# Ten of sixteen comparison rows on ScalarE instead of eight, in the graph-building stage of a GNN kernel

## The chip, the cores and the metric

The kernel runs on one core of a Trainium2 chip. The metric is the device time of one execution in microseconds (us), median over runs; lower is better.

## What is computed

Four graph networks in a row over 6250 nodes and 100000 edges, each with a residual and a layer norm. All of them reduce to products of a feature matrix with one of two dense 6250 x 6250 matrices: W (sum of edge weights between two nodes) and C (number of edges between them).

```python
edge_index = jnp.stack([src, dst])          # dst is sorted
x = _layernorm(x + L0(x, edge_index, edge_weight, ...))   # three GCN layers: need W
x = _layernorm(x + L1(x, src, dst, ...))                  # SAGE: needs C
x = _layernorm(x + L2(x, edge_index, ...))                # five GRU steps: need C
x = _layernorm(x + L3(x, edge_index, ...))                # one GCN layer: needs C
```

## The kernel before

**Building the matrices** (`build_adjacency`). The edges are cut into NB = 49 batches of 2048, in an order ORDER that rises nearly with dst. An edge's cell (its place in the matrix) may occur twice in a batch, and then only one of the copies may be added, with the sum. So each batch is compared with itself: its 2048 keys stand in one row `krow` on all partitions, and for each of the 16 tiles j ("rows" in this text) the keys from tile j on are compared with the 128 keys of tile j, one per partition. Row j has (16 - j) * 128 elements, so row 0 has 2048 and row 15 has 128; row 6 has 1280 and row 7 has 1152. The results are masks `Eq`.

- VectorE (DVE) does rows 0 to DVE_ROWS - 1 in `compare`, one instruction each (L433). Before, DVE_ROWS is 8. Then it makes the one-hot matrices (L438, L443), masks the diagonal blocks of rows 0 to 7 (L450, the *first mask*), weights (L452), and masks the diagonal blocks of rows 8 to 15 (L455, the *second mask*), for which it waits for ScalarE's rows.
- ScalarE (ACT) does the other rows, each in two passes: square of the difference (L273, `distance`) and relu of one minus that (L281, `equality`). After a batch it waits until VectorE has done its rows (`row_used`), issues the load of the keys of the batch after next (L258), and goes on with the next batch.
- TensorE (PE) sums with the masks (L505, L508) and the one-hots (L511), once both masks are there.
- VectorE's `merge` (L463 to L472) turns the sums into the values and the addresses of the batch. It stands behind `compare` of the following batch.
- GpSimd (POOL) then issues 16 indirect DMAs per batch that add the values into W in HBM (L556, *adds*), each of 128 cells; ahead of a batch a small instruction, L531. The adds of all 49 batches into W come first, 782 in all, then in a second pass 782 into C.
- SyncE (SP) zeroes W and C at the start (L228), in zones of 512 columns, and GpSimd waits for the zones that a batch needs.

**The layers** (`run_layers`) follow on the same engines when `built` is set (L483). SP waits for that (L743) and streams the matrix through a ring of 9 buffers (L735); PE multiplies (L849). One stage goes over the matrix in four sweeps of 4, 3, 3 and 3 groups of 512 columns, 49 chunks each. In the first stage each of sweeps 0, 1 and 2 waits for the adds into W that touch its columns (L746), the last for all; in the first stage on C the same holds with the adds into C. Since dst is sorted and grows with the square of a uniform number, a column bound c covers the share sqrt(c / 6250) of the edges; worked out with the inputs and ORDER, sweep 0 needs the first 29 of the 49 batches, sweep 1 37, sweep 2 45 and sweep 3 all. Each sweep ends with L867 where a node adds itself.

Of the kernel before, what the change touches and what calls it, by code (L numbers as in the profile page):

```python
# [33 lines left out]
TB = 16  # L34
# [13 lines left out]
ORDER = [0] + [4 * g + u for g in range((NB - 5) // 4) for u in (2, 4, 1, 3)]  # L48
ORDER += [b for u in (0, 1) for b in range(len(ORDER) + u, NB - 1, 2)] + [NB - 1]
KEY_BIT = 0x50000000  # L50
DVE_ROWS = TB // 2

BANK = 512
UC = 4
# [95 lines left out]
def build_adjacency(nc, io, sems, persist, take, at, psum, c_added):  # L150
# [35 lines left out]
    total, more = take(P, [3, TB], F32), take(P, [TB], F32)  # L186
    apart = take(P, [2, (TB - DVE_ROWS) * P], BF16)
    mask = take(P, [TB], I32)
    names = "rows_in edges_in key_used ramps ident_set zero_set key_set keys_out far_set far_turned zones_set row_used " \
            "equal_set own_set apart_set late_rows batch_counted cell_set dve_step merged hot_set dump_zeroed x_pad_set needed_set needed_turned"  # L190
    s = {n: sems(n) for n in names.split()}
# [5 lines left out]
    def row_start(j):  # L197

        return j * EQ_PAIR if j < TB // 2 else (TB - 1 - j) * EQ_PAIR + (j + 1) * P
# [46 lines left out]
    def scalar(act):  # L246
# [17 lines left out]
        act.wait_ge(s["key_used"], 1)  # L264
        late = TB - DVE_ROWS

        def distance(b, u):

            j, slot = DVE_ROWS + u, b % 2
            n = b * late + u  # L270
# [5 lines left out]
        def equality(b, u):  # L276

            j, slot = DVE_ROWS + u, b % 2
            at = row_start(j)
# [59 lines left out]
    def vector(dve):  # L339
# [86 lines left out]
        def compare(b, slot):  # L426

            dve.wait_ge(row_in[slot], 16 * (b // 2 + 1))
            if b >= 2:
                dve.wait_ge(s["batch_counted"], b - 1)  # L430
            for j in range(DVE_ROWS):
                at = row_start(j)
                ins = dve.tensor_scalar(Eq[:, slot, at:at + (TB - j) * P], krow[:, slot, j * P:],  # L433
                                        keyf[:, b * TB + j:b * TB + j + 1], None, ALU.is_equal, ALU.add,
                                        accum_out=total[:, b % 3, j:j + 1])
            ins.then_inc(s["row_used"], 1)
            high, weighted = ohv[:, slot, :, 1, :], ohv[:, slot, :, 0, :]
            dve.tensor_tensor(high, psRamp[:, 0:CHUNKS].unsqueeze(1).to_broadcast([P, TB, CHUNKS]),  # L438
                              dhi[:, b * TB:(b + 1) * TB].unsqueeze(2).to_broadcast([P, TB, CHUNKS]),
                              ALU.is_equal).then_inc(s["hot_set"], 1)  # L440
            if b >= 1:
                dve.wait_ge(s["batch_counted"], b)
            dve.tensor_tensor(ohl, psRamp.unsqueeze(1).to_broadcast([P, TB, P]),  # L443
                              dlo[:, b * TB:(b + 1) * TB].unsqueeze(2).to_broadcast([P, TB, P]), ALU.is_equal)
            dve.wait_ge(s["row_used"], b + 1)

            half = TB // 2
            near = Eq[:, slot, 0:half * EQ_PAIR].rearrange("p (r f) -> p r f", f=EQ_PAIR)[:, :, 0:P]
            far = Eq[:, slot, EQ_FAR:EQ_FAR * (half + 1)].rearrange("p (r f) -> p r f", f=EQ_FAR)[:, :, 0:P]
            dve.tensor_tensor(Et[:, slot, 0:half, :], near, psUpto.unsqueeze(1).to_broadcast([P, half, P]), ALU.mult)  # L450
            dve.wait_ge(s["hot_set"], b + 1)
            dve.tensor_tensor(weighted, high, psW[:, b * TB:(b + 1) * TB].unsqueeze(2).to_broadcast([P, TB, CHUNKS]),  # L452
                              ALU.mult)
            dve.wait_ge(s["late_rows"], (b + 1) * (TB - DVE_ROWS))
            dve.tensor_tensor(Et[:, slot, half:, :], far, psUpto.unsqueeze(1).to_broadcast([P, half, P]),  # L455
                              ALU.mult).then_inc(s["equal_set"], 1)

        def merge(b, slot):
# [13 lines left out]
            dve.tensor_tensor(idx[:, at], mask, spare0[:, b % 2 * TB:(b % 2 + 1) * TB], ALU.bitwise_xor).then_inc(s["cell_set"], 1)  # L472

        compare(0, 0)
        for b in range(NB):
            if b + 1 < NB:
                compare(b + 1, (b + 1) % 2)
            merge(b, b % 2)
            if b == 0:
                conflicts()  # L480
# [1100 lines left out]
```

## Time and profile before

| | us |
|---|---|
| median of 3 runs (5507.01 to 5510.31) | 5510.14 |
| the profiled execution | 5502.16 |
| its span, first to last instruction | 5500.3 |
| busy: PE / DVE / ACT / POOL | 4752.6 / 1804.3 / 1189.9 / 2479.1 |

The span is that of the instructions; about 2 us of the execution's time lie outside it. The granted TensorE clock is 0.907 of full speed on average. The program has two parts that overlap: the build, until about 1100 us on VectorE and until about 3041 us on GpSimd, and the layers, from 1100 us to the end on TensorE. Idle time of an engine costs something only where another engine then waits for it.

### The profile page before, as it was taken

To read this page: it belongs to the slowest core of one execution; us is meant where nothing else is said; L and a number is where in the kernel's file an instruction comes from. 1 tells how busy PE (TensorE), PEld (TensorE's weight loads), DVE (VectorE), ACT (ScalarE), POOL (GpSimd) and SP (SyncE) were. 2 spreads that over 40 slices of the span, in tenths; PEclk is the share of its full clock that TensorE was granted. 3 is DMA by queue.
4 is the path that set the end of the run, shared out by engine and by line. 5 is a ranking of instruction groups with operands and counts; after the bars stand their busy time and mean duration, and the time that the engine had idled before them with its cause. 6 is when DMAs were issued, how large, how long until landed. Compare 5 with 4: busy or idle time off the path is not lost. (4 is left out here: it accounts for less than half of the span.)

```text
span 5500.3 us, 77896 instructions
## 1 busy us (share of the span) xinstructions
PE 4752.6 (86%) x25659; PEld 2555.6 (46%) x25659; DVE 1804.3 (33%) x3215; ACT 1189.9 (22%) x2478; POOL 2479.1 (45%) x1704
## 2 busy tenths in 40 slices
PE   3544545599699999999999899899999999999999
PEld 3544544544244444444454444444444444444444
DVE  9999999900001000110050211302113021130642
ACT  4555555411011111111120101202102021120320
POOL 3888888878878888888888100000000000000000
PEclk7555555599899999999999999999999999999999
DMA  9999993399699999999989787585775857758477
GB/s 359 369 365 336 341 302 48 31 336 285 179 287 300 274 301 288 296 276 298 288 232 266 225 272 238 154 297 191 244 252 180 299 185 252 244 184 298 144 229 249
DMA packets 717098, 1402.13 MB, mean 255 GB/s; under 512 B 268372, under 2 KB 356264, under 8 KB 691880
## 3 DMA queue, kind: packets, MB, share of 16 engines
q1 hardware_dynamic: 477388, 1342.89, 73.0%
q0 software_dynamic: 225216, 0.70, 7.9%
q10 hardware_dynamic: 14364, 56.99, 2.7%
q8 instruction: 58, 0.95, 0.1%
q14 instruction: 72, 0.59, 0.0%
HBM read 1160.09 MB, written 240.25 MB: 255 GB/s over the span
## 5 line engine op out<-in xcount | busy, mean ns | idle before, releaser
L849 PE MATMUL psum<-arena 128*128 128x512 f16 (+3 forms) x14014 | 3666.9, 422 | 103.9 <-issue 51.9
L849 PEld LDWEIGHTS psum<-arena 128*128 (+2 forms) x14014 | 1668.2, 123 | 2040.4 <-issue 961.9
L556 POOL DMA_INDIRECT W_adj<-arena x782 | 1211.1, 1549 | 279.2 <-issue 259.8
L556 POOL DMA_INDIRECT C_adj<-arena x782 | 1213.5, 1552 | 238.4 <-issue 238.4
L711 POOL TENSOR_TENSOR arena<-arena 128x512 f32 (+1 forms) x13 | 21.5, 1651 | 1716.6 <-DVE arena L1247 1716.6
L433 DVE TENSOR_SCALAR_CACHE_REDUCE arena<-arena 128x2048 bf16<-128x2048 f32 (+7 forms) x392 | 709.4, 1875 | 0.0
L505 PE MATMUL psum<-arena 128*128 (+1 forms) x6664 | 225.0, 167 | 545.3 <-DVE arena L455 523.4
L505 PEld LDWEIGHTS psum<-arena 128*128 128x128 bf16 x6664 | 214.3, 104 | 560.4 <-issue 506.6
L1443 DVE COPY arena<-psum 128x512 f32<-128x512 f32 (+1 forms) x39 | 23.2, 653 | 1174.0 <-PE psum L867 1174.0
L273 ACT ACTIVATE arena<-arena 128x1024 bf16<-128x1024 f32 (+7 forms) x392 | 298.4, 773 | 453.0 <-DVE arena L433 439.0
L1445 DVE TENSOR_SCALAR arena<-psum,arena 128x512 f32<-128x512 f32 x30 | 21.9, 748 | 1038.9 <-PE psum L849 1038.9
L511 PE MATMUL psum<-arena 128*128 128x98 f32 x1568 | 311.3, 390 | 1.5 <-issue 1.4
L1156 ACT ACTIVATE arena<-arena 128x128 f32 x432 | 127.7, 307 | 828.1 <-PE psum L849 808.1
L511 PEld LDWEIGHTS psum<-arena 128*128 128x128 f32 x1568 | 304.2, 302 | 1.6 <-issue 1.2
L281 ACT ACTIVATE arena<-arena 128x1024 bf16<-128x1024 bf16 (+7 forms) x392 | 297.5, 759 | 0.0
L1171 ACT ACTIVATE arena<-psum,arena 128x512 f32<-128x512 f32 (+1 forms) x48 | 28.5, 644 | 1062.5 <-PE psum L849 1062.5
L709 POOL COPY arena<-arena 128x512 f32 (+1 forms) x13 | 8.0, 614 | 502.1 <-DVE arena L1247 502.1
L802 PE MATMUL psum<-arena 128*128 (+1 forms) x260 | 139.4, 619 | 18.0 <-DVE arena L1342 8.8
L1364 DVE SCALAR_TENSOR_TENSOR arena<-psum,arena 128x512 f32 (+1 forms) x52 | 39.0, 751 | 310.5 <-ACT arena L1077 310.5
L804 PE MATMUL psum<-arena 128*128 (+1 forms) x260 | 135.0, 601 | 0.0
L1087 ACT ACTIVATE arena<-arena 128x128 f32 (+1 forms) x147 | 43.4, 307 | 403.2 <-PE psum L849 267.5
L508 PE MATMUL psum<-arena 128*128 128x1 bf16 x784 | 125.9, 165 | 1.4 <-issue 1.4
(236 smaller groups left out, 2571.3 us busy)
## 6 DMA issues: line engine op xcount, KB each, us to landing
arena<-C_adj SPq DMA_DIRECT2D x784, 384.0 KB
arena<-W_adj SPq DMA_DIRECT2D x294, 768.0 KB
arena<-C_adj SPq DMA_DIRECT2D x392, 512.0 KB
arena<-W_adj SPq DMA_DIRECT2D x147, 1024.0 KB
arena<-C_adj SPq DMA_DIRECT2D x392, 288.0 KB
arena<-W_adj SPq DMA_DIRECT2D x147, 576.0 KB
W_adj<-arena SPq DMA_DIRECT2D x12, 6400.0 KB
W_adj<-arena SPq DMA_DIRECT2D x12, 6144.0 KB
```

What stands on the lines that cost most here:

```text
L273: act.activation(apart[:, u % 2, 0:(TB - j) * P], krow[:, slot, j * P:], ACT.Square, bias=keyf[:, b * TB + j:b * TB + j + 1], scale=-1.0). ...
L281: act.activation(Eq[:, slot, at:at + (TB - j) * P], apart[:, u % 2, 0:(TB - j) * P], ACT.Relu, bias=one[:, 0:1], scale=-1.0, accum_out=tot ...
L433: ins = dve.tensor_scalar(Eq[:, slot, at:at + (TB - j) * P], krow[:, slot, j * P:], keyf[:, b * TB + j:b * TB + j + 1], None, ALU.is_equal ...
L505: pe.matmul(psS[:, slot, 5 * i:5 * i + 4], Eq[:, slot, block_of(j, i)], V[:, ds(b * TB + j, 1), :].rearrange("p a c -> p (a c)"), start=(i ...
L508: pe.matmul(psS[:, slot, 5 * i + 4:5 * i + 5], Et[:, slot, own_at(i), :], ones[:, 0:1], start=False, stop=(i == TB - 1), skip_group_check= ...
L511: ins = pe.matmul(psD[:, 0:2 * CHUNKS], ohl[:, j, :], ohv[:, slot, j].rearrange("p c k -> p (c k)"), start=False, stop=False, skip_group_c ...
L556: return pool.indirect_dma_start(table, bass.IndirectOffsetOnAxis(idx[:, t:t + 1], 0), values[:, t:t + 1], None, compute_op=ALU.add)
L802: pe.matmul(psum[:, 4 + gate, :], gates[:, gate * D:(gate + 1) * D], unit(sum_fm, j), start=True, stop=False)
L804: pe.matmul(psum[:, 4 + gate, :], wt[f"whhT{gate}"], unit(h_fm, j), start=False, stop=True).then_inc(s["probs_in"], 1)
L849: ins = pe.matmul(psum[:, bank + b, 0:width], lhs, ring[:, slot, b * BANK:b * BANK + width], start=begin and part == 0, stop=False, skip_g ...
L1087: act.activation(chunk32[:, slot, :], h_nm[:, at_, :].rearrange("p a f -> p (a f)"), ACT.Copy).then_inc(s["chunk_set"], 1)
L1156: act.activation(chunk32[:, u, :], h_nm[:, ds(i * LAP + (u + 1), 1), :].rearrange("p a f -> p (a f)"), ACT.Copy).then_inc(s["chunk_set"], 1)
```

## The change

VectorE takes rows 0 to 5, ScalarE rows 6 to 15. The first mask covers rows 0 to 7, so it now also reads two of ScalarE's rows and gets a wait for them. Nothing else is changed; buffers, the order of the engines' other work and the layers stay.

```diff
-DVE_ROWS = TB // 2
+DVE_ROWS = 6
@@ compare
             near = Eq[:, slot, 0:half * EQ_PAIR].rearrange("p (r f) -> p r f", f=EQ_PAIR)[:, :, 0:P]
             far = Eq[:, slot, EQ_FAR:EQ_FAR * (half + 1)].rearrange("p (r f) -> p r f", f=EQ_FAR)[:, :, 0:P]
+            dve.wait_ge(s["late_rows"], b * (TB - DVE_ROWS) + half - DVE_ROWS)
             dve.tensor_tensor(Et[:, slot, 0:half, :], near, psUpto.unsqueeze(1).to_broadcast([P, half, P]), ALU.mult)
```

On VectorE, in the first `compare` of the program (lines count one higher behind the new wait, so L450 of before is L451 now), the difference reads:

```order
 L433 TENSOR_SCALAR arena<-arena 128x1536
 L433 TENSOR_SCALAR arena<-arena 128x1408
-L433 TENSOR_SCALAR arena<-arena 128x1280
-L433 TENSOR_SCALAR arena<-arena 128x1152
 L438 TENSOR_TENSOR arena<-psum,arena 128x16x49
 L443 TENSOR_TENSOR arena<-psum,arena 128x2048
-L450 TENSOR_TENSOR arena<-arena,psum 128x1024 [waits row_used]
-L452 TENSOR_TENSOR arena<-arena,psum 128x16x49 [waits hot_set]
-L455 TENSOR_TENSOR arena<-arena,psum 128x1024 [waits late_rows]
+L451 TENSOR_TENSOR arena<-arena,psum 128x1024 [waits late_rows,row_used]
+L453 TENSOR_TENSOR arena<-arena,psum 128x16x49 [waits hot_set]
+L456 TENSOR_TENSOR arena<-arena,psum 128x1024 [waits late_rows]
```

Two comparisons are gone in each of 49 batches, and the first mask has one more wait.

On ScalarE the first batch began like this before (sizes are the elements per partition):

```order
L273 ACTIVATE arena<-arena 128x1024 [waits key_used]
L273 ACTIVATE arena<-arena 128x896
L281 ACTIVATE arena<-arena 128x1024 [waits apart_set]
L273 ACTIVATE arena<-arena 128x768 [waits late_rows]
L281 ACTIVATE arena<-arena 128x896 [waits apart_set]
```

and it begins like this now:

```order
L273 ACTIVATE arena<-arena 128x1280 [waits key_used]
L273 ACTIVATE arena<-arena 128x1152
L281 ACTIVATE arena<-arena 128x1280 [waits apart_set]
L273 ACTIVATE arena<-arena 128x1024 [waits late_rows]
L281 ACTIVATE arena<-arena 128x1152 [waits apart_set]
L273 ACTIVATE arena<-arena 128x896 [waits late_rows]
L281 ACTIVATE arena<-arena 128x1024 [waits apart_set]
```

Its two largest rows come first, ahead of those it had.

## Rows read from the trace of the kernel before

**Rows 1.** Windows, all engines: busy us (instructions) in each stretch, clock, DMA share, GB/s.
```profile
400.00:600.00 200.00, 102.09 (x1704) 99.35 (x1702) 199.07 (x250) 111.72 (x224) 165.22 (x114) 0.58 1.11 339
2000.00:2300.00 300.00, 295.76 (x846) 144.08 (x845) 16.23 (x40) 40.33 (x131) 250.58 (x171) 1.00 1.01 294
```
**Rows 2.** Timeline of PE: start, us, engine, line, operation, count [idle before, releaser].
```profile
1107.14 170.72 PE L849 MATMUL psum<-arena 128*128 128x512 f32 x392 [4.79 <-DMA arena<-W_adj]
...
1281.26 126.34 PE L849 MATMUL psum<-arena 128*128 128x512 f32 x294
...
1462.20 8.03 PE L849 MATMUL psum<-arena 128*128 128x512 f32 x13 [51.92 <-issue]
```
**Rows 3.** Timeline of PE at the first stage on C, last sweep.
```profile
3046.84 13.35 PE L849 MATMUL psum<-arena 128*128 128x512 f16 x70 [30.80 <-DMA arena<-C_adj]
```
**Rows 4.** Windows for L556 alone: POOL busy (adds), clock, DMA share, GB/s.
```profile
723.30:931.50 208.20, 173.44 (x112) 0.58 0.68 163
931.50:1158.50 227.00, 174.41 (x112) 0.66 0.50 123
```
**Rows 5.** Timeline of POOL around every 112th add into W.
```profile
723.40 1.55 POOL L556 DMA_INDIRECT W_adj<-arena  x1 [6.70 <-issue]
...
931.56 1.55 POOL L556 DMA_INDIRECT W_adj<-arena  x1 [0.30 <-issue]
...
1139.02 1.55 POOL L556 DMA_INDIRECT W_adj<-arena  x1 [0.16 <-issue]
1158.57 1.55 POOL L556 DMA_INDIRECT W_adj<-arena  x1 [18.00 <-issue]
...
1369.21 1.55 POOL L556 DMA_INDIRECT W_adj<-arena  x1 [2.77 <-issue]
```
**Rows 6.** Timeline of POOL: first batch, second batch, last add of the 45th.
```profile
70.37 1.72 POOL L556 DMA_INDIRECT W_adj<-arena  x1 [13.26 <-DVE arena L472]
...
106.09 0.19 POOL L531 TENSOR_TENSOR arena<-arena 128x1 f32<-128x1 f32 x1 [6.27 <-DMA W_adj<-arena]
...
1454.61 1.55 POOL L556 DMA_INDIRECT W_adj<-arena  x1 [0.30 <-issue]
```
**Rows 7.** Timeline of DVE: rows 6 and 7 of batch 0, end of its merge.
```profile
39.43 1.54 DVE L433 TENSOR_SCALAR_CACHE_REDUCE arena<-arena 128x1280 bf16<-128x1280 f32 x1
40.90 1.41 DVE L433 TENSOR_SCALAR_CACHE_REDUCE arena<-arena 128x1152 bf16<-128x1152 f32 x1
42.23 0.97 DVE L438 TENSOR_TENSOR arena<-psum,arena 128x784 f32<-128x784 f32 x1
...
69.89 0.18 DVE L472 TENSOR_TENSOR arena<-arena 128x16 int32<-128x16 int32 x1
```
**Rows 8.** Timeline of one batch in mid-build: DVE's L443 twice, PE's end.
```profile
606.52 2.28 DVE L443 TENSOR_TENSOR arena<-psum,arena 128x2048 f32<-128x2048 f32 x1
617.32 6.76 PE L511 MATMUL psum<-arena 128*128 128x98 f32 x32
628.16 2.28 DVE L443 TENSOR_TENSOR arena<-psum,arena 128x2048 f32<-128x2048 f32 x1
```
**Rows 9.** Timeline of ACT in the same batch, first and last instruction.
```profile
606.26 2.08 ACT L273 ACTIVATE arena<-arena 128x1024 bf16<-128x1024 f32 x2 [9.19 <-DVE arena L433]
...
618.42 0.18 ACT L281 ACTIVATION_READ_ACCUMULATOR arena<-arena 128x1 f32 x1
```
**Rows 10.** Groups by form, ACT, 60 to 1080 us: busy us, mean ns | idle before.
```profile
L281 ACT ACTIVATE arena<-arena 128x1024 bf16<-128x1024 bf16 x47 | 53.2, 1132 | 0.0
...
L281 ACT ACTIVATE arena<-arena 128x128 bf16<-128x128 bf16 x47 | 18.1, 385 | 0.0
```
**Rows 11.** Waits of SP, 750 to 1110 us: total, times, longest.
```profile
SPq L743 <- DVE arena L483: 287.5, 1, 287.5
```
**Rows 12.** Windows, all engines, while the layers stream W.
```profile
1130.00:1140.00 10.00, 10.00 (x25) 4.44 (x24) 0.00 (x0) 0.93 (x3) 8.62 (x7) 1.00 1.07 395
1390.00:1400.00 10.00, 10.00 (x25) 4.41 (x24) 0.00 (x0) 0.00 (x0) 8.62 (x7) 1.00 0.32 32
1450.00:1460.00 10.00, 0.00 (x0) 0.00 (x0) 0.00 (x0) 0.00 (x0) 8.56 (x7) 0.50 0.28 28
```

## The prediction

> **What bounds the kernel now.** I read the windows first. In the build VectorE is busy 199 of 200 us and GpSimd 165 of 200; later GpSimd keeps that density (251 of 300) while VectorE is nearly idle [rows 1]. That looks like a build bound by VectorE, and it is not. The windows of L556 alone, cut at every 112th add, give 208.2 us for 112 adds, which is seven batches of 16: 29.74 us a batch [rows 4]. VectorE's period, from L443 to L443 of the next batch, is 628.16 - 606.52 = 21.64 us [rows 8]. So VectorE runs ahead of the adds, and GpSimd is full in its own way: each add takes 1.55 us and 0.30 us follow it. Only its first batch waits for VectorE [rows 6].
>
> Then the timeline of PE, where the time is decided. The layers begin at 1107.14; the first two sweeps run to 1277.9 and 1407.6, and PE then stands still for 51.9 us until 1462.20 [rows 2]. The last add of the 45th batch is issued at 1454.61 [rows 6], and sweep 2 needs 45 batches: PE waits for GpSimd. It waits once more, 30.8 us until 3046.84, for the last sweep of the first stage on C [rows 3], which needs all 1564 adds. No wait behind that one is for an add. So the end of the kernel is the end of GpSimd's adds plus work that this change leaves alone. VectorE's gain counts only where it moves GpSimd.
>
> Last the timeline of GpSimd at its gaps. Between the first and the second add of batches 7, 14, 21, 28, 35 and 42, so after every 112 adds, it may pause. The idle time there is 6.70 us while SP zeroes (723.40), 0.30 us, so nothing, at 931.56 when the DMA is quiet, 18.00 us at 1158.57, and 2.77 us at 1369.21 while chunks stream evenly [rows 5]. The 18 us one falls into the burst with which SP fills the ring of nine 1 MB buffers: it may issue only when the build ends, at about 1102, and waits 287.5 us for that [rows 11], and until past 1150 the DMA moves some 395 GB/s [rows 12]. I read this as a pause for the adds in flight to land, which is long when they queue behind the burst. The fixed spacing speaks for it; the trace has only one such pause in a burst.
>
> **The change, part by part.**
>
> VectorE loses rows 6 and 7. Start to start they take 40.90 - 39.43 = 1.47 and 42.23 - 40.90 = 1.33 us [rows 7], so 2.80 us per batch and a period of 18.84. Over 49 batches its part of the build ends 137.2 us earlier.
>
> ScalarE gains two rows in two passes. An L281 of 1024 takes 1.132 us and one of 128 takes 0.385 [rows 10], so 0.107 us per 128 elements: 1.345 us for 1280 and 1.239 for 1152. L273 is like it, which makes 2 x 2.58 = 5.2 us, or 5.0 with the overlap of neighbours, on top of 618.60 - 606.26 = 12.3 [rows 9]: 17.3 us. That is dear per row, 5.0 against VectorE's 2.8 us. The Trainium skill ("ScalarE: Activation LUTs", Rules for kernel authors) advises VectorE over ScalarE for such plain arithmetic, and budgets about 0.3 us plus 0.83 ns per element; as an estimate that is 1.36 and 1.26 us and a batch of 17.5. With the page's figure too the batch stays under 18.84. ScalarE starts a batch 0.6 us after VectorE's rows of the one before (L443 at 606.52 less about 0.9 for L438, against 606.26, [rows 7 to 9]), so it ends at 17.9 of 18.84 us. Bounds: the two rows cost at least 4 x 1.13 = 4.5 us, and at most in proportion to tiles (19 more on 36) 6.5 us. At the upper end ScalarE sets a period of 19.4, still far under 29.74, and the build ends 25 us later than said.
>
> The new wait of the first mask. Rows 6 and 7 are ScalarE's first, done some 6.5 us after it starts (the two passes and the square of row 8). VectorE comes to the mask after six rows that are each longer than 1.47 us, 8.8 at least, and L438 and L443, 3.1 more. Behind the wait stand the weights, the second mask, the merge and so GpSimd, but it is over by 5 us or more each time. Cost: nothing. The second mask waits for all ten rows. Counted from the end of VectorE's rows of the batch before, L443 starts at 0.9 + 18.84 = 19.7 us and the mask stands 2.2 us and more behind it; ScalarE is done at 17.9.
>
> PE ends batch work at 624.08, and VectorE comes to L443, which waits for it, at 628.16; 2.80 us earlier is 625.36, so 1.3 us remain [rows 8]. No cost; and if it had one, it would be the build's, which has 10.9 us a batch to spare against the adds.
>
> GpSimd's start. Two `compare` stand ahead of the first merge: 2 x 2.80 = 5.60 us. The first add comes at 64.8 in place of 70.37. The zones were ready at 57.1 (70.37 - 13.26), so nothing else stops it. The waits of batches 1 and 2 are for the landing of the batch before (6.3 us, [rows 6]) and move along. **Gain 5.6 us.** Bounds: 0 if the early landings, among the zeroing, are later; 5.6.
>
> The pause after 112 x 5 adds. The layers now begin at 1107.14 - 137.2 = 969.9; the 29 batches that sweep 0 needs are in by then (batch 28's last add stands 14 adds of 1.85 behind 931.56, at 957.5, less 5.6). Sweep 0 takes 170.7 us, to 1140.6. Its loads end earlier: sweep 1's were over by about 1391, since 1390 to 1400 moved only 32 GB/s, 16 us before PE's 1407.6 [rows 2, 12]. So the DMA is quiet from about 1124, because sweep 1 must wait for batch 36. GpSimd comes to its pause 5.6 us before the old place, at 1135, 11 us into the quiet. The pause should be that of 931.56: 0.30 in place of 18.00. **Gain 17.7 us.** Bounds: with the loads still running, 2.77, a gain of 15.2; in the burst, none.
>
> The burst itself moves to 965, where 0.30 at 931.56 (926 now) is already past. Sweep 1 waits for batch 36, whose last add stands 30 adds of 1.855 behind 1158.57, at 1214.2, less 23.3 now; PE follows such an add by 7.6 us (1454.61 and 1462.20, [rows 2, 6]), so near 1199, and ends near 1326; the next pause, at 1369.21 less 2.5 and less 23.3, is at 1343: quiet too. **Gain 2.5 us.** Sweep 2 and everything on C keep their place relative to the adds.
>
> Sum: 5.6 + 17.7 + 2.5 = 25.8 us. Against the profiled execution, 5502.16 - 25.8 = 5476.4; that execution is 8 us under the median of the runs, so against the median 5510.14 - 25.8 = 5484.3 us. PE waits much more in the first stage (for batch 36 as well) and is at the lower clock when it starts again, but it was so before sweep 2 also (0.50 at 1450, [rows 12]), and the adds, not PE, decide.
>
> **Rivals.**
>
> *A, the 18 us belong to the burst, not to the count.* Too many adds in flight stop GpSimd wherever the burst is; then they only move to about 1005. Gain 5.6 + 2.5 = 8.1: 5502.0 us. For it: one case only. Against: the gap sits exactly at the 112th add. Chance 0.17.
>
> *B, the pause meets a part of the streaming*, because ScalarE or PE ends the build later by over 11 us: 5.6 + 15.2 + 0 to 2.5, so 5487 to 5489; if the build ended only 10 to 25 us earlier than before, it would still meet the burst. With A's mechanism in part, up to 5498. Chance 0.10.
>
> *C, slower.* As A, and the backlog also stops GpSimd in the new burst at sweep 1, which is filled from empty where it followed seamlessly before: 18 us more. Then -5.6 - 2.5 + 17.7 = +9.6, 5519.7 us. It decides from a third pause of over 8 us. Against it: sweep 2 starts from empty before, and the adds behind 1462 keep their 1.85 us. Chance 0.04.
>
> *D, the saving is hidden wholly*: the usual reading, "VectorE is not the bound", with the pause unchanged and the early gain lost among the zeroing: 5508 to 5512. Chance 0.04.
>
> **How the numbers follow.** The forecast has 0.65, with 5478 to 5492 for the sum and the spread of the medians. B adds 0.10 up to 5498. A is within 0.2% (11 us, about what a measurement of this kernel can tell from no change), D too; C lies at the edge of slower. Faster: 0.65 + 0.10 less a little for spread: 0.74. Same: 0.17 + 0.04 + 0.01: 0.22. Slower: 0.04. The range reaches from 5476 to 5504, so it holds A and leaves out C and D and what goes beyond the sum.
>
> **What would show it.** VectorE's L443 should come every 18.8 us; ScalarE's group of a batch should take 17 to 18 us. The first add should start near 65 us and PE's first L849 near 970. The pause behind the 560th add should be under 1 us near 1135, with PE waiting near 1141 to 1199 and 1326 to 1436. The wait for C should end near 3021. It is wrong if a gap of 10 us or more stands elsewhere among the adds, or if PE has no wait for C at all, so that another chain sets the end.

## The result, and the profile after

The changed kernel takes 5477.36 us (median of 5 runs, 5475.12 to 5479.92) against 5507.13 us of the kernel before (5505.86 to 5510.31): ratio 0.9944, 95% interval 0.993 to 0.9959, 29.8 us faster by the medians. The profiled execution took 5476.16 us, 26.0 us less than that of before (5502.16); 25.8 were forecast.

The timeline of PE in the changed kernel (start, us, then what stood idle before), which answers to [rows 2] and [rows 3]:

```profile
969.73 170.15 PE L850 MATMUL psum<-arena 128*128 128x512 f32 x392 [5.29 <-ACT arena L1088]
...
1196.36 129.12 PE L850 MATMUL psum<-arena 128*128 128x512 f32 x294 [52.91 <-issue]
...
1434.14 46.02 PE L850 MATMUL psum<-arena 128*128 128x512 f32 x103 [105.98 <-issue]
...
3021.89 38.44 PE L850 MATMUL psum<-arena 128*128 128x512 f16 x227 [31.71 <-DMA arena<-C_adj]
```

The layers start 137.4 us earlier, and PE loses most of it standing: 52.9 us before sweep 1 and 106.0 before sweep 2, where one wait of 51.9 was before, so 107.0 of the 137.4. At the last sweep of the first stage on C the gain is down to 3046.84 - 3021.89 = 24.95 us.

The timeline of GpSimd, for [rows 5] and [rows 6]:

```profile
65.00 1.72 POOL L557 DMA_INDIRECT W_adj<-arena  x1 [7.92 <-DVE arena L473]
...
716.86 1.55 POOL L557 DMA_INDIRECT W_adj<-arena  x1 [3.77 <-issue]
...
924.99 1.55 POOL L557 DMA_INDIRECT W_adj<-arena  x1 [0.30 <-issue]
...
1133.11 1.55 POOL L557 DMA_INDIRECT W_adj<-arena  x1 [0.30 <-issue]
...
1341.24 1.55 POOL L557 DMA_INDIRECT W_adj<-arena  x1 [0.30 <-issue]
...
3015.92 1.55 POOL L557 DMA_INDIRECT C_adj<-arena  x1 [0.30 <-issue]
```

The pauses of 18.00 and 2.77 us in batches 35 and 42 are gone: 0.30 us stand there, as ahead of every add. The windows around them (PE, PEld, DVE, ACT, POOL busy, clock, DMA share, GB/s), for [rows 12]:

```profile
1000.00:1010.00 10.00, 10.00 (x24) 4.38 (x24) 0.00 (x0) 0.93 (x3) 8.47 (x6) 1.00 1.08 398
1116.00:1126.00 10.00, 10.00 (x25) 4.39 (x24) 0.00 (x0) 0.00 (x0) 8.17 (x7) 1.00 0.33 33
1130.00:1140.00 10.00, 10.00 (x27) 4.51 (x26) 0.00 (x0) 0.08 (x1) 8.62 (x7) 1.00 0.23 2
```

The burst is where the layers start now (398 GB/s at 1000), and when GpSimd comes to batch 35 the DMA moves 2 GB/s. In the burst itself GpSimd is not held: its adds go on at their pace (six begin in these 10 us). Rival A had put a stop of 18 us there.

One batch of mid-build on VectorE and ScalarE, for [rows 8] and [rows 9]; two timelines:

```profile
595.14 2.35 DVE L433 TENSOR_SCALAR_CACHE_REDUCE arena<-arena 128x2048 bf16<-128x2048 f32 x1
...
613.89 2.35 DVE L433 TENSOR_SCALAR_CACHE_REDUCE arena<-arena 128x2048 bf16<-128x2048 f32 x1
```

```profile
607.37 2.51 ACT L273 ACTIVATE arena<-arena 128x1280 bf16<-128x1280 f32 x2 [1.14 <-DVE arena L433]
...
624.80 0.19 ACT L281 ACTIVATION_READ_ACCUMULATOR arena<-arena 128x1 f32 x1
```

VectorE's period is 613.89 - 595.14 = 18.75 us, ScalarE's batch 624.99 - 607.37 = 17.62. ScalarE waits 1.14 us for VectorE where it waited 9.19.

### The profile page after: what moved, and what is told of

Same layout as the page of the kernel before. It is cut to its first block and busy times, and to the rows that moved or that the text cites. A ratio compares the mean times of both kernels' runs of the same rounds, so it can differ in the third digit from the quotient of the medians.

```text
span 5474.4 us, 78043 instructions
## 1 busy us (share of the span) xinstructions
PE 4734.8 (86%) x25659; PEld 2543.3 (46%) x25659; DVE 1667.5 (30%) x3019; ACT 1444.8 (26%) x2772; POOL 2476.9 (45%) x1704
## 3 DMA queue, kind: packets, MB, share of 16 engines
q0 software_dynamic: 225216, 0.70, 7.9%
## 5 line engine op out<-in xcount | busy, mean ns | idle before, releaser
L506 PE MATMUL psum<-arena 128*128 (+1 forms) x6664 | 211.2, 167 | 431.1 <-DVE arena L456 427.3
L433 DVE TENSOR_SCALAR_CACHE_REDUCE arena<-arena 128x2048 bf16<-128x2048 f32 (+5 forms) x294 | 572.3, 2009 | 0.0
L273 ACT ACTIVATE arena<-arena 128x1280 bf16<-128x1280 f32 (+4 forms) x490 | 426.6, 880 | 73.7 <-DVE arena L433 57.4
L281 ACT ACTIVATE arena<-arena 128x1280 bf16<-128x1280 bf16 (+4 forms) x490 | 424.1, 866 | 0.0
L803 PE MATMUL psum<-arena 128*128 (+1 forms) x260 | 139.2, 618 | 18.0 <-DVE arena L1343 8.8
L805 PE MATMUL psum<-arena 128*128 (+1 forms) x260 | 135.1, 601 | 0.0
```

Of the source, the lines that this page charges most:

```text
L273: act.activation(apart[:, u % 2, 0:(TB - j) * P], krow[:, slot, j * P:], ACT.Square, bias=keyf[:, b * TB + j:b * TB + j + 1], scale=-1.0). ...
L281: act.activation(Eq[:, slot, at:at + (TB - j) * P], apart[:, u % 2, 0:(TB - j) * P], ACT.Relu, bias=one[:, 0:1], scale=-1.0, accum_out=tot ...
L506: pe.matmul(psS[:, slot, 5 * i:5 * i + 4], Eq[:, slot, block_of(j, i)], V[:, ds(b * TB + j, 1), :].rearrange("p a c -> p (a c)"), start=(i ...
L803: pe.matmul(psum[:, 4 + gate, :], gates[:, gate * D:(gate + 1) * D], unit(sum_fm, j), start=True, stop=False)
L805: pe.matmul(psum[:, 4 + gate, :], wt[f"whhT{gate}"], unit(h_fm, j), start=False, stop=True).then_inc(s["probs_in"], 1)
```

## The experiments

The burst's start below is SP's first load of W in the timeline of SP. "Pause" is the idle time between the first and the second add of a batch. In the edits, `added[0]` counts the landed adds into W of the batches 0, 2, 4 and so on, and `added[1]` those of the batches 1, 3, 5 and so on, so `PER_BATCH * 18` of `added[0]` is the landing of batch 34. A line of the timeline of SP is marked SPq.

**1. The kernel before, burst moved behind the pause.**

```diff
                     for u in range(2):
                         sp.wait_ge(added[u], least[u])
+                    if k == 0 and sweep == 0:
+                        sp.wait_ge(added[0], PER_BATCH * 18)
```

> The kernel before (eight rows on VectorE), only SP holds its first load of W until the adds of batch 34 have landed, so that the burst that fills the ring starts near 1140 and not at 1102. My theory (GpSimd pauses at every seventh batch until its adds in flight have landed, and the 18 us were the backlog of the burst): the pause in batch 35 falls to 1 to 4 us, the layers start 38 us later than before, and the kernel is 14 to 18 us faster than before all the same, though VectorE and ScalarE do nothing else. Rival A (the burst's backlog itself stops GpSimd, wherever it falls): a stop of about 18 us follows inside batches 36 to 38, gain 0 to 2 us. Rival D (it is VectorE's earlier end that gives the time): no gain, or a loss from the later start of the layers.

Measured: 5489.62 us (5486.14 to 5492.85) against 5508.08; ratio 0.9968 (0.9955 to 0.998), 18.5 us faster. The timelines of SP at the burst's start and of GpSimd in batch 35:

```profile
1139.74 5.11 SPq L735 DMA_DIRECT2D arena<-W_adj  x8
...
1138.48 1.55 POOL L556 DMA_INDIRECT W_adj<-arena  x1 [0.16 <-issue]
1140.34 1.55 POOL L556 DMA_INDIRECT W_adj<-arena  x1 [0.30 <-issue]
```

The burst starts at 1139.74 and PE at 1144.83, the pause is that of a quiet DMA (0.30), and no stop of the adds over 1 us follows it until batch 42 (2.65 us). So a kernel with VectorE and ScalarE as before, and layers that start 38 us later, takes most of the gain. Rivals A and D fall here.

**2. The changed kernel, burst put back ahead of the pause.** As above on the changed kernel, with `added[1], PER_BATCH * 17`.

> The changed kernel (six rows on VectorE), only SP holds its first load of W until the adds of batch 33 have landed, near 1103, so that the burst stands 30 us ahead of the pause in batch 35, much as before the change. My theory: the pause is 16 to 19 us again, the one in batch 42 is back at 2 to 3 us, and of the gain only the 5 us of the earlier first add remain: 5 to 8 us faster than before. Rival A: the stop comes at the backlog, thus in batch 34 or 35 also, but then the unheld kernel would have had it near 1000. Rival D (the shorter build gives the time): the gain of nearly 30 us stays, since VectorE is as fast as in the changed kernel.

Measured: 5499.23 us (5493.04 to 5503.44), ratio 0.9985 (0.9976 to 0.9994), 8.9 us faster than before. 5 to 8 were expected. The burst's start, and batch 35:

```profile
1105.82 42.52 SPq L736 DMA_DIRECT2D arena<-W_adj  x18
...
1134.36 1.55 POOL L557 DMA_INDIRECT W_adj<-arena  x1 [0.16 <-issue]
1153.09 1.55 POOL L557 DMA_INDIRECT W_adj<-arena  x1 [17.18 <-issue]
```

With six rows on VectorE the 17 us are back as soon as the burst stands 30 us ahead of the pause, and two thirds of the gain are gone. In batch 42 it is 1.64 us, a little under the 2 to 3 expected. Rival D falls here too.

**3. The changed kernel, burst 60 us ahead of the pause.** The same with `added[0], PER_BATCH * 17`.

> The changed kernel, only SP holds its first load of W until the adds of batch 32 have landed, near 1073, 60 us ahead of the pause in batch 35 (30 us ahead in the run with the burst put back, 100 with seven rows). My theory: the backlog is worked off by then, the pause is 2 to 5 us, the one in batch 42 under 1 us or up to 3: 5479 to 5484. If the pause were a matter of SP's hold or of PE's late start, it would cost as the run with the burst put back, near 5499.

Measured: 5484.27 us (5482.1 to 5488.41), ratio 0.9959 (0.9944 to 0.9974), at the upper end of the 5479 to 5484 expected. Burst at 1073.92, and

```profile
1132.29 1.55 POOL L557 DMA_INDIRECT W_adj<-arena  x1 [0.16 <-issue]
1136.74 1.55 POOL L557 DMA_INDIRECT W_adj<-arena  x1 [2.89 <-issue]
```

PE starts 109 us later than in the changed kernel here (1078.93). The profiled execution takes 6.8 us more than that of the changed kernel, and the pauses, those of batches 35 (2.9) and 42 (1.2) and the small ones in the zeroing and on C, are 6.7 us longer together. The late start of PE costs nothing.

**4. Seven rows on VectorE.**

```diff
-DVE_ROWS = 6
+DVE_ROWS = 7
```

(and the two buffers of squares by the running number of the row, also in run 6).

> Seven rows on VectorE, nine on ScalarE (its two buffers of squares are taken in turn over the whole program, because nine is odd). My theory: first add 2.7 us earlier than before, build ends near 1035, the pause in batch 35 falls 100 us behind the burst and is 2 to 3 us, the one in batch 42 under 1: 19 to 23 us faster than before, which is three quarters of the whole change for half of the move. A rival in which the gain is in proportion to VectorE's saved time gives half, 13 to 15 us.

Measured: 5490.34 us (5486.96 to 5495.4), ratio 0.997 (0.9959 to 0.998), 17.7 us faster, less than the 19 to 23 expected; the interval spans 11 to 23 us and so does not decide against the half, 13 to 15, by time. The trace shows what the gain is made of: first add at 67.81 (2.56 earlier), burst at 1038.43, pause in batch 35 1.93 us, none in batch 42. By the last add, which stands at 3024.29, it is 16.7 us ahead of the profile of before. These three terms make 21.1 us; the 4 us that are missing are in the zeroing and on C, where the pauses sum to 27.9 us against 23.7.

**5. Merge of batch 0 ahead of the second compare.**

```diff
         compare(0, 0)
+        merge(0, 0)
         for b in range(NB):
             if b + 1 < NB:
                 compare(b + 1, (b + 1) % 2)
-            merge(b, b % 2)
+            if b:
+                merge(b, b % 2)
```

> The changed kernel, only VectorE merges batch 0 before it compares batch 1, so that the first adds need one compare and not two. My theory (the end is the end of the adds, which begin with the first merge): the first add comes at 57 to 58 in place of 65.0, bounded by the zones at 57; VectorE waits 10 us for PE once, so batch 1's values come near 96, 3 us after GpSimd wants them: 4 to 8 us faster than the changed kernel, 5470 to 5473. If the pause in batch 35 then meets the end of sweep 0's loads, 2 us less. Rival: the landings of batches 1 and 2 amid the zeroing take up what the first batch gains: as the changed kernel.

Measured: 5479.69 us (5477.29 to 5483.05), ratio 0.9952 (0.9938 to 0.9965): as the changed kernel, so the 4 to 8 us expected did not come, and the rival has it right. The first add does come 7 us earlier,

```profile
57.96 1.72 POOL L559 DMA_INDIRECT W_adj<-arena  x1 [0.75 <-DVE arena L473]
```

but batch 3 starts at 164.90 against 167.94 (the waits for values and landings of batches 1 and 2 take 4 back), and the last add, at 3018.85, is 2.9 us later than the changed kernel's: the other 3 us, and 2.9 more, are lost behind it, among others in the pauses of batches 7, 14 and 21 (14.4 against 13.5 us), in those on C (14.3 against 11.2) and in batches 29 and 30, which take 1.1 us longer together. A few microseconds at the start do not arrive whole at the end.

**6. Five rows on VectorE.** `DVE_ROWS = 5`.

> Five rows on VectorE, eleven on ScalarE. ScalarE's batch should be 20 us and set the period at 20 to 21 us, so the build ends near 1040 to 1060 and the layers start 70 to 90 us later than in the changed kernel. My theory: that costs nothing by itself, the first add comes 2.5 to 3.2 us earlier, near 62, and the pause in batch 35 falls 75 to 95 us behind the burst and is 2 to 3 us, 42's under 1: 5475 to 5481, as the changed kernel. Rival (the length of the build counts): 10 us or more slower than the changed kernel.

Measured: 5483.78 us (5476.48 to 5486.47), ratio 0.9954 (0.994 to 0.9967), 3 us above the 5475 to 5481 expected. ScalarE is the build's bound now; the window at 400 to 600 us and the wait of VectorE for it, 100 to 900 us:

```profile
400.00:600.00 200.00, 106.43 (x1826) 103.32 (x1827) 164.44 (x205) 191.97 (x308) 164.16 (x113) 0.58 1.12 341
```

```profile
DVE arena L456 <- ACT arena L281: 128.3, 37, 3.9
```

The burst starts at 1070.23, 106 us later than in the changed kernel (1040 to 1060 were expected). The medians are 6 us apart, less than the 10 of the rival, and the last adds 4.5; of these the pauses, 2.53 us in batch 35 and 2.02 in 42 (the latter expected under 1), make 4.0 over the idle time that stands ahead of any add. The first add comes at 63.12, not 62: VectorE has waited 1.3 us for ScalarE ahead of it.

**7. Eight more adds in front.** On the kernel before:

```diff
                 add_column(pool, W_adj, idx, wsum, b * TB + j).then_inc(w_added[b % 2], 16)
+            if b == 0:
+                for j in range(8):
+                    add_column(pool, W_adj, spare0, zero, TB + j).then_inc(s["extra"], 16)
+                pool.wait_ge(s["extra"], 128)
```

(not shown: the new semaphore `extra`, and a wait for it on SP ahead of its load of x).

> The kernel before with eight more adds of zeros to spare cells of W behind batch 0's sixteen, for which GpSimd waits; nothing that the reference sees changes. It asks what the pause is tied to. If to the number of adds (113th, then every 112th): the pause moves eight adds ahead in the program, to batch 34 between its ninth and tenth add, stands at the same time near 1141, so in the burst, and is 18 us again: 5522 to 5526. If to the place in the program (the second add of every seventh batch): it stays in batch 35, now near 1157, 55 us behind the start of the burst, and is 2 to 5 us: the 15 us of the extra adds and 14 us less pause nearly cancel, 5507 to 5513. Under either my account of its length stands: the backlog at its time.

Measured: 5508.81 us (5505.61 to 5510.48) against 5507.21, ratio 1.0002 (0.9992 to 1.0011). The 15 us of the adds are made up for by shorter pauses, as expected under the second reading, but the place was neither: the pauses moved one batch on, to batches 8, 15, 22, 29 and 36. At 1142, where the count would have put it, nothing stands, and in batch 36:

```profile
1142.00 1.55 POOL L561 DMA_INDIRECT W_adj<-arena  x1 [0.30 <-issue]
1143.86 1.55 POOL L561 DMA_INDIRECT W_adj<-arena  x1 [0.30 <-issue]
...
1186.65 1.55 POOL L561 DMA_INDIRECT W_adj<-arena  x1 [0.16 <-issue]
1191.81 1.55 POOL L561 DMA_INDIRECT W_adj<-arena  x1 [3.61 <-issue]
```

So the adds pass through the burst (start 1102.46) without a stop even with VectorE as before, and the pause 86 us behind it is short. What fixes its place stays open: it is not the plain number of adds (it came 137 adds after the first, not 113), nor the instruction alone. Two things are on record: in the pass into C the pauses stand in batches 7, 14, 21 and so on of that pass in all runs, this one too, so the count begins anew there; and here the first pause stands 113 adds behind the wait for the eight adds, as it stands 113 adds behind the start of a pass elsewhere. That the wait restarts the count was not tested; the waits for landings ahead of batches 1 and 2 do not.

**8. and 9. Both kernels once more.**

> The kernel before once more, for a second profile. My theory: the pause in batch 35 is 17 to 19 us again, the others differ by 1 to 3 us each with where the landings stand at their moment, and their sum explains most of the spread of its runs: 5503 to 5511. If the 18 us were a chance of one execution, it would be gone here.

> The changed kernel once more, on the same chip as the kernel before. My theory: pause in batch 35 and 42 at 0.3 again, first add near 65, 5476 to 5482, so 26 to 30 us faster than before.

Measured: before 5509.18 us (5501.69 to 5512.76), with ratio 0.9998 (0.9989 to 1.0007) to the other runs of it on that chip, and after 5479.81 us (5476.38 to 5483.01), ratio 0.9947 (0.9933 to 0.996), 28.9 us faster. The pause in batch 35 of the kernel before is there again:

```profile
1138.89 1.55 POOL L556 DMA_INDIRECT W_adj<-arena  x1 [0.16 <-issue]
1158.95 1.55 POOL L556 DMA_INDIRECT W_adj<-arena  x1 [18.51 <-issue]
```

and 0.3 us in the changed one. The profiled executions differ by 5510.19 - 5480.28 = 29.9 us. Between the two profiles of the kernel before, 8.0 us apart, the pauses differ by 4.1 us in sum: they explain half of it, not most.

## Why the prediction was right

**The bound.** In all eleven profiles the time of the execution is the start of the last add plus a constant: 5502.16 - 3040.96 = 2461.2 before, 5476.16 - 3015.92 = 2460.2 after, and between 2458.4 and 2463.4 in all, while the layers started anywhere from 970 to 1145 us. PE waited for the adds into C in each (30.8 and 31.7 us above, 33 to 38 in runs 1 to 9), so the adds and not PE set the end. Runs 1 and 3 show it from the other side: PE 38 and 109 us later, no cost.

**VectorE and ScalarE.** Period 18.75 us (18.84 said), ScalarE 17.6 (17.3 said: the two rows cost 5.3 us, as added up before the overlap of neighbours was taken off), end of its batch ahead of VectorE's rows by 1.1 us. The first mask waits for nothing, as argued, and for PE VectorE waits once in 100 to 900 us, 1.5 us.

**The start.** 5.37 us for 5.6. But the loss in run 5 shows that this term is less sure than it was taken for: it is passed on only as far as later landings allow.

**The pause.** 17.7 us (18.00 to 0.30), as said; run 1 gives it without the move of rows and run 2 takes it away with the move. Its length against the distance from the burst's start: at once 0.3 (run 1), 30 us behind it 17.2 (run 2), 38 and 39 us 18.5 and 18.0 (before), 60 us 2.9 and 2.5 (runs 3, 6), 86 us 3.6 (run 7), 101 us 1.9 (run 4), 169 us 0.3 (after). That is the shape of a backlog that builds up and is worked off. The 2.5 us in batch 42 were right as well.

That the pause is for the adds in flight can be read from the packets. An add makes 144 of them in the queue of GpSimd (225216 packets for 1564 adds). In the kernel before, the packets of that queue that had begun by 1140.6, where the pause starts, and by 1158.57, where it ends (number, MB, share of the 16 engines):

```profile
q0 software_dynamic: 79705, 0.32, 13.6%
q0 software_dynamic: 80784, 0.32, 13.5%
```

561 adds had been issued, and 561 x 144 = 80784: at the start of the pause 1079 packets, seven and a half adds, had still to begin, and GpSimd went on when none had. By the ends of the packets, in all eleven profiles and at all twelve such places of each, W and C, at most one add was unfinished when the next one began. At the other places more may be. In the burst of the changed kernel, by 1014.1:

```profile
q0 software_dynamic: 70204, 0.28, 12.7%
```

497 adds had been issued, so 9.5 of them had still to begin, and the next add followed at 1014.19, after 0.30 us like any other. So the number in flight does not stop GpSimd (rival A), the pause is the wait until they are through, and the backlog of the burst sets its length: in the changed kernel the time from the start of an add to the end of its last packet (the packets counted off in the order of their ends) rises from 2.6 us ahead of the burst to 19 us at 29 us behind its start, and is 5 us at 57. A load of instructions is not what it waits for: in the 18 us of that pause no packet of the kind instruction began.

**What the sum left out or mis-sized.** PE did keep its place relative to the adds on C (24.95 us earlier, the last add 25.04), but the adds did not keep their own pitch. By the starts of the batches the gain is 28.0 us when the adds into W end, 2.2 us above the sum: 1.2 because batches 34 and 35 are no longer late (their starts stood 30.07 and 30.56 us behind the one before, not 29.73; about half of that is not the burst's, for in run 1, where they come ahead of it, they stand at 30.02 and 30.01), the rest in the pauses of the zeroing. On C 3.0 us of it are lost again: 1.3 in the landing waits ahead of its second and third batch, most of the rest in the pauses, which sum to 11.2 us against 8.9. So the agreement of the two profiled executions, 26.0 us for 25.8, is in part luck. The profiles give 26.0 and 29.9 us, the medians 29.8 and 28.9; the pauses in the zeroing and on C, which differ between executions (23.7 us in one profile of before, 27.1 in the other), are of that size. So the likely size of the change is 29 us, 3 above the sum.

Against the median the sum gave 5484.3 us, and 5477.36 were measured: in the range of 5476 to 5504, but near its lower end, and just under the 5478 to 5492 that were given for the sum alone. Of the 6.9 us between them 3.0 come from the median of before, 5510.14 of three runs and 5507.13 of five, and 4.0 from the gain, 29.8 for 25.8.

## What to carry to other kernels

An engine that is 99% busy is not the bound if the next one has its own, longer period: compare the periods, then look which wait ends last. Making the faster one faster still can pay through what it triggers: here the end of the build releases a burst of loads, and the time came from the burst leaving the one spot at which GpSimd's DMA stream pauses. If such a burst can be held or let go early for free, try that first; run 1 took 18 us with one wait, without touching VectorE or ScalarE.

## What the runs showed of the hardware that was not expected

A stream of indirect DMAs with accumulation from GpSimd paused once in 112 adds (7 batches of 16) until at most one of the adds before was unfinished: 0.3 us with the DMA quiet (once 1.8, in batch 29 of run 7, at 105 GB/s), 0.3 to 3.8 with some 300 GB/s of loads, 3.2 to 7.4 among the zeroing at 330 to 370, and 17 to 18.5 us 30 to 39 us after a burst of loads began. Between these places up to 9.9 adds were in flight (run 3), with no idle time over 0.32 us between two adds of a batch. Outside that spot the two batches in a burst took at most 1.2 us longer together. Eight adds and one wait more in front shifted the spot by a whole batch.
